# Edge stage of a four-layer graph network: source numbers reach all partitions by a TensorE product from SBUF, and both edge sums share one PSUM bank

## What is computed

```python
src, dst = (edge_index[0], edge_index[1])
pair_emb = jnp.concatenate([node_emb[src], node_emb[dst]], axis=-1)
h = jax.nn.relu(pair_emb @ W1 + b1)
interaction = h @ W2 + b2
gate = jax.nn.sigmoid(interaction @ Wg + bg)
gated = interaction * gate
summed = jax.ops.segment_sum(gated, src, num_segments=N)
counts = jax.ops.segment_sum(jnp.ones((src.shape[0],), dtype=gated.dtype), src, num_segments=N)
pooled = summed / jnp.maximum(counts, 1.0)[:, None]
```

## Time and profile before

| | |
|---|---|
| median of 3 runs | 4126.92 us (4124.71 to 4128.42) |
| span of the profiled execution | 4931.5 us (no other time of this execution is recorded) |
| edge stage in it | 2130 to about 4888 us |
| mean granted TensorE clock of it | 0.686 |
| TensorE (PE) busy | 3795.1 us, 77% of the span |
| VectorE (DVE) busy | 2361.5 us, 48% |
| ScalarE (ACT) busy | 1755.3 us, 36% |
| GpSimd (POOL) busy | 1565.7 us, 32% |

### The profile page before, as it was taken

One profiled execution on the slowest core, in us unless ns is written; L12 is line 12 of the kernel. 1 busy time (PEld: TensorE's weight loads), 2 busy tenths in 40 slices (PEclk: granted clock), 3 DMA queues, 4 the chain that ended last, 5 costly groups with the idle time before them and its releaser, 6 DMA issues. The chain is left out here.

```text
span 4931.5 us, 130776 instructions
## 1 busy us (share of the span) xinstructions
PE 3795.1 (77%) x40587; PEld 3225.1 (65%) x40588; DVE 2361.5 (48%) x7074; ACT 1755.3 (36%) x3946; POOL 1565.7 (32%) x1680
## 2 busy tenths in 40 slices
PE   6872688888798989947777777777777777777776
PEld 3441344444598989847777777777777777777776
DVE  9999999999502111143333333333333333333334
ACT  7861688888400000122222222222222222222223
POOL 0000100000000000055555555555555555555552
PEclk9985899999899999955555555555555555555555
DMA  1000122222598888621111111111111111111111
GB/s 39 4 2 9 75 104 104 104 104 114 225 336 307 314 308 316 229 51 41 40 39 39 39 40 40 38 39 39 39 41 40 39 40 40 40 41 39 39 41 31
DMA packets 182945, 444.91 MB, mean 90 GB/s; under 512 B 53003, under 2 KB 111635, under 8 KB 157039
## 3 DMA queue, kind: packets, MB, share of 16 engines
q1 hardware_dynamic: 131475, 387.96, 22.9%
q0 software_dynamic: 51040, 53.55, 5.2%
q10 hardware_dynamic: 252, 1.08, 0.1%
HBM read 356.29 MB, written 86.12 MB: 90 GB/s over the span
## 5 line engine op out<-in xcount | busy, mean ns | idle before, releaser
L1132 POOL DMA_INDIRECT x<-b_table,gidx x1568 | 1484.3, 947 | 1258.7 <-DVE x L943 819.5
L1432 ACT ACTIVATE x<-ps,b1col 64x256 f32<-64x256 f32 x880 | 411.2, 467 | 1735.1 <-remote 1534.8
L1804 PE MATMUL ps<-w2cat,x 65*128 65x128 f32 x3520 | 854.7, 423 | 13.2 <-issue 12.1
L1816 PEld LDWEIGHTS ps<-x 128*128 128x128 f32 x3520 | 805.3, 332 | 37.8 <-issue 22.8
L1816 PE MATMUL ps<-x 128*128 128x65 f32 x3520 | 800.1, 404 | 32.4 <-issue 21.4
L1804 PEld LDWEIGHTS ps<-w2cat,x 65*128 65x128 f32 x3520 | 801.1, 332 | 26.3 <-issue 14.2
L1784 PE MATMUL ps<-x 128*128 128x64 bf16 x5280 | 465.0, 239 | 447.5 <-issue 429.9
L943 DVE TENSOR_TENSOR x<-ps,x 128x256 f32<-128x256 f32 x440 | 186.8, 425 | 1234.1 <-remote 645.5
L1784 PEld LDWEIGHTS ps<-x 128*128 128x128 bf16 x5280 | 417.9, 138 | 515.9 <-issue 514.4
L1612 PE MATMUL ps<-rows 128*128 128x448 bf16 x2272 | 614.7, 399 | 148.0 <-DVE rows L728 67.2
L1612 PEld LDWEIGHTS ps<-rows 128*128 128x128 bf16 x2272 | 329.0, 145 | 433.7 <-issue 308.7
(11 more groups left out here) (272 smaller groups left out, 2512.6 us busy)
## 6 DMA issues: line engine op xcount, KB each, us to landing
rows<-adjacency SPq DMA_DIRECT2D x90, 1024.0 KB, 5.6
adjacency<-stage SPq DMA_DIRECT2D x50, 1568.0 KB, 5.2
x<-adjacency SPq DMA_DIRECT2D x60, 1024.0 KB, 5.4
x<-src_rows SPq DMA_DIRECT2D x440, 128.0 KB
rows<-adjacency SPq DMA_DIRECT2D x90, 544.0 KB, 4.9
x<-adjacency SPq DMA_DIRECT2D x60, 544.0 KB, 5.5
x<-b_table,gidx POOLq DMA_INDIRECT x1568
key_rows<-x ACTq DMA_DIRECT2D x1, 1024.0 KB, 4.4
```

Source lines behind the costliest of these rows:

```text
L1132: e.indirect_dma_start(out=BGT[:, s, j, :], out_offset=None, in_=b_table, in_offset=bass.IndirectOffsetOnAxis(ap=gidx[:, u * G + j:u * G + ...
L1432: ins = e.activation(pair[:, :, h, :], ps[h * D:(h + 1) * D, u, 0:2 * P].rearrange("p (a n) -> p a n", n=P), ACT.Relu, bias=b1col[h * D:(h ...
L1804: ins = e.matmul(ps[:, 2 + u, j * P:(j + 1) * P], H[0:D + 1, u, j * P:(j + 1) * P], w2cat[:], start=True, stop=True)
L1816: ins = e.matmul(ps[:, 4 + u, 0:D + 1], OS[:, s, j, :], MG[:, u, j, :], start=(j == 0), stop=(j == G - 1))
```

## The change

In the kernel after, the source numbers stay in SBUF (`item_rows`, one row of 512 numbers per item, 128 items to a block). TensorE multiplies that block by a stationary operand that repeats one column of the identity 128 times, which writes row n of the block to every partition of PSUM bank 5 (`spread_ids`). `make_hot_t` reads that bank instead of `SROW`. The product for item i+1 is issued at the head of `edge_rows(i)`, behind the wait for `OT(i)`. The 440 transfers, the DRAM tensor and its store go. As bank 5 is taken, all `sum_edges` write bank 4, so `sum_edges(i)` now waits for `add_sum(i-1)`, and VectorE does `add_sum` before `gated`. `total` and `item_rows` have other places in the same tile.

```diff
-            def make_hot_t(i, rnd, s, first):
+            def make_hot_t(i, s, first):
-                e.wait_ge(srow_landed[s], 16 * rnd + 16)
+                e.wait_ge(ids_ready, i + 1)
                 if not first:
                     e.wait_ge(rows_ready, i - 1)
-                e.tensor_scalar(OT[:, s % 2, :], SROW[:, s, :], part_f[:, 0:1], None,
+                e.tensor_scalar(OT[:, s % 2, :], ps[:, ID_BANK, :], part_f[:, 0:1], None,
                                 ALU.is_equal).then_inc(ot_ready, 1)
...
                     add_b(i - 2, (s + 2) % 4)
-                    make_hot_t(i, r, s, False)
+                    make_hot_t(i, s, False)
+                    add_sum(i - 5)
                     gated(i - 4, s % 2, False)
-                    add_sum(i - 5, (s + 1) % 2)
                     make_hot(i - 1, (s + 3) % 4, False)
...
-            def load_ids(i, s, first):
-                if not first:
-                    e.wait_ge(ot_ready, i - 3)
-                e.dma_start(SROW[:, s, :], src_rows[bass.ds(i, 1), :].to_broadcast([P, G * P])
-                            ).then_inc(srow_landed[s], 16)
...
+            def spread_ids(block, row):
+
+                e.matmul(ps[:, ID_BANK, :], ident_b[:, row].to_broadcast([P, P]), item_rows[:, block],
+                         start=True, stop=True).then_inc(ids_ready, 1)
+
             def edge_rows(i, s, first):
 
                 e.wait_ge(at_ready, i + 1)
                 e.wait_ge(ot_ready, i + 1)
+                if isinstance(i, int):
+                    n = min(i + 1, ITEMS - 1)
+                    block, row = slice(n // P * G * P, (n // P + 1) * G * P), slice(n % P, n % P + 1)
+                else:
+                    n = e.snap(i + 1)
+                    block, row = bass.ds((e.snap(n >> 7) & (ITEM_BLOCKS - 1)) * (G * P), G * P), bass.ds(e.snap(n & (P - 1)), 1)
+                spread_ids(block, row)
                 if not first:
                     e.wait_ge(b_added, i - 1)
...
-                if not first:
-                    e.wait_ge(sum_taken, i)
+                e.wait_ge(sum_taken, i + 1)
                 for j in range(G):
-                    ins = e.matmul(ps[:, 4 + u, 0:D + 1], OS[:, s, j, :], MG[:, u, j, :], start=(j == 0),
+                    ins = e.matmul(ps[:, SUM_BANK, 0:D + 1], OS[:, s, j, :], MG[:, u, j, :], start=(j == 0),
                                    stop=(j == G - 1))
```

More of the change, by code:

```diff
@@ L101 @@
 HALF_SPAN = SPAN // 2
+SUM_BANK, ID_BANK = 4, 5
 assert GR % SPAN == 0
@@ L150, in build_gnn @@
     b_table = nc.dram_tensor("b_table", [NTP * P, D], F32).ap()
-    src_rows = nc.dram_tensor("src_rows", [ITEMS_PAD, G * P], BF16).ap()
     dst_rows = nc.dram_tensor("dst_rows", [2, TRIO * ROW_LEN], BF16).ap()
@@ L290, in build_gnn @@
         src_items = stage_f[:, 0:ITEMS_PAD * G]
-        item_rows = sflat[:, 2 * ITEMS_PAD * G:2 * ITEMS_PAD * G + ITEM_BLOCKS * G * P]
-        total = stage_f[:, ITEMS_PAD * G:ITEMS_PAD * G + NTP * (D + 1)].rearrange("p (t f) -> p t f", f=D + 1)
+        item_rows = sflat[:, 2 * MCOLS - ITEM_BLOCKS * G * P:]
+        total = stage_f[:, ITEMS * G:ITEMS * G + NTP * (D + 1)].rearrange("p (t f) -> p t f", f=D + 1)
+        assert 2 * (ITEMS * G + NTP * (D + 1)) <= 2 * MCOLS - ITEM_BLOCKS * G * P >= 2 * ITEMS_PAD * G
         item_keys = T1[:].rearrange("p a b -> p (a b)").bitcast(I32)[:, 0:ITEM_BLOCKS * G * P]
@@ L309, in build_gnn @@
         AT = ring(4, 3 * D, BF16)
-        SROW = ring(4, G * P, BF16)
         OT = ring(2, G * P, BF16)
@@ L401, in build_gnn @@
         table_out = sem("table_out")
-        srows_out = sem("srows_out")
-        srow_landed = [sem(f"srow_landed{n}") for n in range(4)]
+        ids_ready = sem("ids_ready")
         b_landed = [sem(f"b_landed{n}") for n in range(RING)]
@@ L962, in gated, with add_sum @@
                                 ALU.mult).then_inc(gated_ready, 1)
-            def add_sum(i, u):
+            def add_sum(i):
                 tile_reg = e.snap(e.value_load(tile_tab[0:1, bass.ds(i, 1)], min_val=0, max_val=NTP - 1))
@@ L968, in add_sum @@
                 a = total[:, bass.ds(tile_reg, 1), :].rearrange("p a f -> p (a f)")
-                e.tensor_tensor(a, a, ps[:, 4 + u, 0:D + 1], ALU.add).then_inc(sum_taken, 1)
+                e.tensor_tensor(a, a, ps[:, SUM_BANK, 0:D + 1], ALU.add).then_inc(sum_taken, 1)
             e.wait_ge(total_zeroed, 1)
@@ L976, in _ @@
                     add_b(i - 2, (i - 2) % 4)
-                make_hot_t(i, i // 4, i % 4, i < 2)
+                make_hot_t(i, i % 4, i < 2)
+                if i >= 5:
+                    add_sum(i - 5)
                 if i >= 4:
                     gated(i - 4, i % 2, i < 6)
-                if i >= 5:
-                    add_sum(i - 5, (i - 5) % 2)
                 if i >= 1:
@@ L995, in _ @@
             for i in range(ITEMS - 4, ITEMS):
+                add_sum(i - 1)
                 gated(i, i % 2, False)
-                add_sum(i - 1, (i - 1) % 2)
-            add_sum(ITEMS - 1, (ITEMS - 1) % 2)
+            add_sum(ITEMS - 1)
             e.wait_ge(sum_taken, ITEMS + 1)
@@ L1244, in _ @@
                 load_rounds(layer, 0, TAIL_AT if layer else [0, ROUNDS])
[L1245 to L1248, removed]
                 load_rounds(layer, 1, HEAD_AT)
@@ L1254, in _ @@
                 e.dma_start(b_tiles[:, lo:hi, :], AGG[:, lo:hi, :]).then_inc(table_out, 16)
-            e.wait_ge(srows_out, 16)
-            def load_ids(i, s, first):
-                if not first:
-                    e.wait_ge(ot_ready, i - 3)
-                e.dma_start(SROW[:, s, :], src_rows[bass.ds(i, 1), :].to_broadcast([P, G * P])
-                            ).then_inc(srow_landed[s], 16)
[L1264 to L1268, removed]
             for lo, hi, ready in ((0, ROOT[1], "first_rows"), (ROOT[1], FULL, "final")):
@@ L1408, in _ @@
                 root(f"var2_{g - 1}", 8 * (g - 1), min(8 * g, NTP))
-            e.wait_ge(srows_out, 16)
+            e.wait_ge(item_copied, ITEM_BLOCKS)
             e.activation(total.rearrange("p t f -> p (t f)"), repeat(zero_col[:], NTP * (D + 1)), ACT.Copy
@@ L1806, in interact, with sum_edges @@
                 ins.then_inc(g_ps_ready, 1)
-            def sum_edges(i, s, first):
+            def sum_edges(i, s):
                 u = s % 2
@@ L1820, in _ @@
             e.wait_ge(dve, mark["a_split"])
+            spread_ids(slice(0, G * P), slice(0, 1))
             for i in range(8):
@@ L1827, in _ @@
                 if i >= 3:
-                    sum_edges(i - 3, (i - 3) % 4, i < 5)
+                    sum_edges(i - 3, (i - 3) % 4)
             with e.Fori(2, ITEMS // 4) as rnd:
@@ L1834, in _ @@
                     interact(i - 2, s % 2, False)
-                    sum_edges(i - 3, (s + 1) % 4, False)
+                    sum_edges(i - 3, (s + 1) % 4)
             turn_rows(ITEMS - 1, (ITEMS - 1) % 4, False)
@@ L1838, in _ @@
                 interact(i, i % 2, False)
-                sum_edges(i - 1, (i - 1) % 4, False)
-            sum_edges(ITEMS - 1, (ITEMS - 1) % 4, False)
+                sum_edges(i - 1, (i - 1) % 4)
+            sum_edges(ITEMS - 1, (ITEMS - 1) % 4)
 _INS = ["x", "src", "dst", "L0_gnn_W", "L0_gnn_b", "L1_gnn_U", "L1_gnn_V", "L2_gnn_W", "L2_gnn_b",
```

## The result

The kernel after takes 4291.19 us in the median of 4 runs (4281.03 to 4298.63), the kernel before 4127.67 (4 runs, 4124.71 to 4131.06). The ratio is 1.0395, with a 95% interval of 1.0382 to 1.0408: slower by 163.5 us. Forecast were 4318 us, 191 more than before, in a range of 4290 to 4375 (162 to 247 more).

The account below looks back on a forecast made before the run. TensorE at half clock was taken to bound the edge stage, just ahead of the gathers. The product adds 440 x 0.43 = 188 us and nothing comes off: 4127 + 188 = 4315, set at 4318 us, range 4290 to 4375.

Parts of the forecast that it names:

- TensorE's price: Edge stage, new 512-column product on PE: 0.43 us an item by columns, 188 us over 440 items; 0.53 if its load is exposed.
- The pauses are not in the timed runs: Edge stage, PE's issue gaps: put down to the profiler; 809 us over 440 items of 4.43 us, against 804.6 extra span.
- What bounds before: Kernel before, edge stage: TensorE at half clock sets 4123 us, the gathers 4115, so PE bounds by 8 us only.
- TensorE's sum: Kernel before: 2130 us to the edge stage, 1949 for 440 items of 4.43, 43.5 for the end; together 4123 us.
- The gathers' sum: POOL's indirect transfers: 1568 at 1.25 us from 2109 to 4069, some 3 us to land, 43.5 for the end; 4115 us.
- up to 12 us: Doubt about the bound: if the timed kernel before ran at the gathers' pace by up to 12 us, 4303 us after.
- The transfers bound nothing: The 440 transfers of source numbers in the edge stage: hidden, so removing them gains 0; the gathers gain nothing either.
- VectorE's read and the hand-over: `make_hot_t` reading PSUM: 0.69 us for 0.35, hidden; its new wait on PE also 0, with `gated` slack 0.75 us.
- The place called the tightest: VectorE's `add_b`, done by 5.4 us, before PE's `turn_rows` at 5.95: slack about 0.5 us, so cost 0.
- Rival C: Hand-over through the one id bank costs time: 4400 to 4500 us, at worst 4620; chance 0.08.
- One bank: `sum_edges(i)` waiting for `add_sum(i-1)` on the single sum bank: cost 0, since it already waits for `gated(i)` just behind.
- Rival B: Edge stage: the dense product raises PE's clock, the gathers then bound, about 4115 us, up to 4130; chance 0.12.

## Why the prediction was right, point by point

**TensorE's price.** Forecast 0.43 us an item from the 448-column row. In the profile after it is 0.43, from 3117.95 to 3118.38; its load of weights is hidden, as chosen, though it takes 0.25 us and not the 0.10 that the upper bound used. Over the whole stage the product costs 188.6 us where 188 were forecast (the table above), and half the width bears the slope out.

**The pauses are not in the timed runs.** Inferred from 809 against 804.6 us, and right: before, profiled again, has a span of 4120.3. The item of 4.43 us was real too. But the prediction read "no gap for two items on end" from 3447.09 to 3456.35, and that is wrong: the first of them takes 4.83 us and stands in the view with

```profile
3448.16 0.66 PE L1795 MATMUL ps<-ident,x 128*128 128x128 f32 x2 [0.23 <-DVE x L943]
```

PE waited there for `add_b`. Only the second item is without a gap. The cause given for the pauses, the profiler, was wrong as far as it meant every profile: twelve later profiles have none of them, before itself again, three more kernels with the 440 transfers, and eight without (or with four of them). What stopped PE in that one execution stays open.

**What bounds before.** This is the step that failed, and it is the term that was mis-sized: the order of the two limits. The prediction put TensorE at 4123 and the gathers at 4115, TensorE ahead by 8 us, and so let nothing come off the product's 188 us. The runs have TensorE at 4104 and the kernel at 4127, with the gathers ahead by 22 us.

TensorE's sum was 19 us too long. About 10 of them are its first product, which stood at 2130.0 in the disturbed profile and stands at 2120.4 in that of the run with three gathers (2119.6 to 2127.4 in all the other profiles). About 10 more are the stage itself: 440 full items and the end make 1992.5 us, and 1982.2 were measured, since the first and last items lack parts of the round.

The gathers' sum was too short. The quiet steps give 20.07 / 16 = 1.254 us, which was rounded to 1.25. Unrounded, 1568 of them are 1967 us in place of 1960, and the sum is 4122, level with TensorE's 4123. Over the whole stage the mean is 1.260, and the 1974.5 us are 14 more than the 1960. Rounding is 7 of these. In the trace of before profiled again six steps of 2.1 to 2.6 us, which come every 224 gathers where POOL's loop turns, make 7 more. From the first gather to the end the kernel takes 2019.9 us, where the prediction summed 2006. With the product twice it takes 2019.5.

So 188 us of product less some 22 us of cover make 166; measured were 163.5. The prediction had this doubt as "up to 12 us" and reached 4303 with it. That the measured 4291 is in the range is luck: it lies 1 us from the lower end, which had been set as far again below 4303.

**The transfers bound nothing.** Right: the run without 436 of them is at 0.9992.

**VectorE's read and the hand-over.** The read takes 0.75 us, not 0.69. It costs nothing that shows: `gated` is ready 1.1 us before PE wants it (0.75 was forecast). The place called the tightest, `add_b` ahead of `turn_rows`, had 1.5 us (3117.52 to 3119.04) where 0.5 was forecast. Rival C, with its hundreds of microseconds, is out by the run with the unread product; the intervals leave at most 17 us of it.

**One bank.** Forecast 0, measured between 0 and 7 us.

**Rival B, the clock.** It didn't come in: 0.50 in the whole stage in the profile of the kernel after. But the reason against it, that the new product adds only a tenth to the stream, was weak, and so was the other one, the two items without a gap. One half product more turns it, and the time it then gives is that of the rival, the gathers' limit (4121 and 4125 against the 4115 to 4130 worked out). The rule of the Trainium skill quoted with it ("TensorE: Matmul & The Clock Gate", "Why this matters for your kernels") doesn't describe this stage: in the profile of before with three gathers PE was busy for 1935.8 of 1938 us at a granted clock of 0.50. By its own words continuous work would have given the full clock. What brought the clock up here for most of the time wasn't a greater busy share (1623 of 1959 us with one and a half products) but half a bf16 product of 512 columns more in the same stream. Why that turns it is not shown.

## What to carry to other kernels

When two limits are within a per cent of each other, the cost of work added to one of them is its price less the gap to the other, so measure both floors, by leaving out work on each side (here a quarter of the gathers), before pricing the change; a price per transfer has to come from the whole stage, not from a quiet start, and isn't to be rounded when it is taken 1568 times. If a profile's span is well over the timed runs, take a second profile: it may be that execution and not the kernel, and it can hide which engine is late. And if TensorE bounds a stage at a granted clock of 0.50 although it is always busy, try adding a dense product before taking work off: here an unneeded one of 256 columns bought back all that the needed one had cost (back to the kernel before, not below it), and with a quarter of the gathers left out an unneeded one of 512 columns bought 508 us.

## What the runs showed of the hardware that was not expected

- TensorE can be busy 99.9% of a stage at 1.2 GHz. Its stream was, for each item, 12 bf16 products of 64 columns and 18 rows of f32 products: 2 of 128 columns, 8 of 128 columns with 65 of 128 partitions, and 8 of 65 columns behind a load of 128. Which of these keeps the clock down was not tested.
- More work can take less time. One product of 512 columns an item on top of that stream left the mean granted clock of the stage at 0.50, one and a half raised it to 0.77, two to 0.82.
- With one product the clock went either way. In the profile of after it stayed at 0.50. In that with the unread product it was 1.00 for 20 us near the start, in that with three gathers for 75 us, and then it fell for good. Without the product and with half of it, it never rose in the stage. The four runs of the kernel after lie in the order of their mean granted clocks (4281.0 us at 0.717 to 4298.6 at 0.713), so this is a likely part of their spread. Another part is where the stage begins, 2119.6 to 2127.4 us in the undisturbed profiles. No run isolates either.
